# Two self-attentions: in PE's turn the score matmuls come ahead of the reciprocals' product and the transposition of the normalised tile

## The reference

```python
def _layernorm(x, axis=-1, eps=1e-05):
    m = jnp.mean(x, axis=axis, keepdims=True)
    v = jnp.var(x, axis=axis, keepdims=True)
    return (x - m) / jnp.sqrt(v + eps)
...
        q = _apply_rope(q, cos, sin)
        k = _apply_rope(k, cos, sin)
...
        scores = jnp.einsum('bhqd,bhkd->bhqk', q, k) / jnp.sqrt(jnp.float32(HEAD_DIM))
        causal = jnp.where(jnp.tril(jnp.ones((S, S), jnp.float32)) == 0, -1000000000.0, 0.0)
        scores = scores + causal
        attn = jax.nn.softmax(scores, axis=-1)
        out = jnp.einsum('bhqk,bhkd->bhqd', attn, v)
...
    x = x + _L0_attn_ref(_layernorm(x, axis=-1), L0_attn_wq, L0_attn_bq, L0_attn_wk, L0_attn_bk, L0_attn_wv, L0_attn_bv, L0_attn_wo, L0_attn_bo)
    x = x + _L0_xattn_ref(_layernorm(x, axis=-1), ctx_1024, ctx_1024, L0_xattn_igate_kernel, L0_xattn_igate_bias, L0_xattn_fgate_kernel, L0_xattn_fgate_bias, L0_xattn_outnorm_scale)
    x = x + _L0_ffn_ref(_layernorm(x, axis=-1), L0_ffn_sW1, L0_ffn_sb1, L0_ffn_sW2, L0_ffn_sb2, L0_ffn_rW1, L0_ffn_rb1, L0_ffn_rW2, L0_ffn_rb2, L0_ffn_gW, L0_ffn_gb)
    x = x + _L1_attn_ref(_layernorm(x, axis=-1), L1_attn_Wq, L1_attn_Wk, L1_attn_Wv, L1_attn_Wo)
    x = x + _L1_xattn_ref(ctx_1024, _layernorm(x, axis=-1), L1_xattn_gamma_x, L1_xattn_beta_x, L1_xattn_gamma_l, L1_xattn_beta_l, L1_xattn_Wq, L1_xattn_Wkv, L1_xattn_Wo)
    x = x + _L1_ffn_ref(_layernorm(x, axis=-1), L1_ffn_phi, L1_ffn_W, L1_ffn_b)
```

## Time and profile before

| | |
|---|---|
| median of 3 runs | 2063.2 us (2062.44 to 2063.45) |
| the profiled execution | 2060.2 us, span of its instructions 2058.1 us |
| self-attention of layer 0 | about 57 to 256 us; PE busy 176.09, DVE 170.35, ACT 156.30, POOL 130.45 of 199 us |
| self-attention of layer 1 | about 824 to 1031 us; PE busy 179.08, DVE 148.60, ACT 161.14, POOL 98.68 of 207 us |
| busy over the whole span | PE 1863.2, DVE 1458.5, ACT 1446.9, POOL 1123.8 us |

### The profile page before, as it was taken

How to read it: one execution, slowest core, us unless ns; L and a number is a source line. 1 busy time by engine, 2 the same in 40 slices (tenths; PEclk the granted TensorE clock), 3 DMA queues, 4 the chain that set the end, 5 groups by cost and what they waited for, 6 DMA issues and landing times. The chain is left out here.

```text
span 2058.1 us, 62588 instructions
## 1 busy us (share of the span) xinstructions
PE 1863.2 (91%) x23443; PEld 1475.0 (72%) x23505; DVE 1458.5 (71%) x3895; ACT 1446.9 (70%) x4203; POOL 1123.8 (55%) x1453
## 2 busy tenths in 40 slices
PE   5899798699999998889879999767999999999998
PEld 3566565577777776566568888656888888888787
DVE  7799768666566665677756666578777777777567
ACT  5688767688888887688768888566666666666532
POOL 5677447688888888545333333147444544445520
PEclk9999999899999999899999999899999999999999
DMA  3011010322222222000011111100000000000101
GB/s 98 28 48 41 13 33 3 83 73 73 74 72 77 73 73 62 23 2 2 2 34 32 33 33 33 58 26 4 5 15 18 5 16 5 16 15 3 56 8 39
DMA packets 60619, 72.47 MB, mean 35 GB/s; under 512 B 10264, under 2 KB 38696, under 8 KB 60064
## 3 DMA queue, kind: packets, MB, share of 16 engines
q1 hardware_dynamic: 51104, 64.29, 10.5%
q10 hardware_dynamic: 9216, 4.20, 0.7%
HBM read 51.43 MB, written 4.44 MB: 27 GB/s over the span
## 5 line engine op out<-in xcount | busy, mean ns | idle before, releaser
L1094 POOL TENSOR_TENSOR ff_hl<-ff_hid,ff_hh 128x512 fp32r<-128x512 f32 x272 | 350.2, 1302 | 69.1 <-ACT ff_hh L1335 61.9
L1954 POOL TENSOR_TENSOR sm_zsum<-sm_zsum,sm_logits 128x512 f32<-128x512 f32 x120 | 154.6, 1289 | 271.2 <-ACT sm_logits L1980 269.5
L1257 DVE TENSOR_TENSOR ff_hid<-ff_p_b,ff_gates 128x512 f32<-128x512 f32 x240 | 164.4, 686 | 148.6 <-ACT ff_p_b L1324 146.4
L1997 ACT ACTIVATE sm_sT<-sm_p_s 128x512 f32<-128x512 f32 x128 | 69.5, 595 | 217.3 <-PE sm_p_s L1790 217.3
L613 ACT ACTIVATE at_pr<-at_p_s,at_small 128x64 f32<-128x64 f32 x512 | 154.9, 329 | 61.1 <-DVE at_small L499 61.1
L1335 ACT ACTIVATE ff_hh<-ff_hid 128x512 fp32r<-128x512 f32 x272 | 169.9, 625 | 39.1 <-DVE ff_hid L1257 38.9
L1324 ACT ACTIVATE ff_p_b<-ff_p_h,early_b 128x512 f32<-128x512 f32 x240 | 156.9, 654 | 19.3 <-PE ff_p_h L1151 18.0
L1966 POOL TENSOR_TENSOR sm_logits<-sm_logits,sm_peak 128x512 f32<-128x512 f32 x128 | 163.1, 1296 | 12.5 <-ACT sm_comb L2015 11.9
L1804 PE MATMUL sm_p_l<-g_phi,g_xnT 128*128 128x256 f32 x512 | 142.3, 404 | 26.5 <-ACT sm_logits L2025 25.3
L582 POOL TENSOR_TENSOR at_kblk<-at_kT,early_heads 128x512 f32<-128x512 f32 x128 | 131.7, 1049 | 28.9 <-PE at_p_s L479 26.7
L1838 PE MATMUL sm_p_y<-sm_w,sm_sT 128*32 128x128 f32 x4096 | 125.4, 274 | 9.1 <-ACT sm_combT L1987 8.4
(11 more groups left out here) (305 smaller groups left out, 5610.1 us busy)
## 6 DMA issues: line engine op xcount, KB each, us to landing
ff_gates<-kept_gates SPq DMA_DIRECT2D x120, 256.0 KB, 3.1
xa_kturn<-xa_ksin SPq DMA_DIRECT2D x128, 64.0 KB, 2.0
at_turned<-at_terms SPq DMA_DIRECT2D x64, 64.0 KB, 1.9
sm_w<-in_w_soft SPq DMA_DIRECT2D x8, 512.0 KB, 3.5
early_whole<-in_L_ffn_rW SPq DMA_DIRECT2D x30, 128.0 KB, 2.6
early_xs<-in_x ACTq DMA_DIRECT2D x32, 64.0 KB, 1.9
ld_ctx<-in_ctx ACTq DMA_DIRECT2D x32, 64.0 KB, 2.1
x_kept<-early_xs SPq DMA_DIRECT2D x1, 2048.0 KB, 7.4
```

Source lines behind the costliest of these rows:

```text
L1094: eng.tensor_tensor(hl[:, q, :], hid[:, q, :], hh[:, q, :].bitcast(F32), ALU.subtract).then_inc(h_split, 1)
L1257: dve.tensor_tensor(h, p_b[c % 2][:, :], gates[:, n % GR, :], ALU.mult).then_inc(scaled, 1)
L1954: pool.tensor_tensor(z, z, logits[:, j % RING_L, :, :], ALU.add).then_inc(summed, 1)
```

## The change

In PE's turn the block of the scores moves in front of the block of L460 and that of L300. No instruction, wait or buffer is added or removed; every wait stays with its block. It is in the code of both layers.

```diff
                     mm.then_inc(v_done, 1)
-                k, v = t, u
-                if has(k):
-
-
-                    pe.wait_ge(inverted, k + 1)
-                    if has(k - 1):
-                        pe.wait_ge(oT_made, k)
-                    pe.matmul(p_o[:, P:2 * P], inv[:, v % 2, :, :].rearrange("p h d -> p (h d)"), g["ident"][:, :],
-                              start=True, stop=True).then_inc(inv_turned, 1)
-                k, v = t - 3, (u - 1) % 2
-                if has(k):
-                    if has(t - 2):
-                        pe.wait_ge(x_made, t - 1)
-                    norm.pe_transpose(pe, k, v, p_y[:, P:2 * P])
                 k, v = t + 2, (u + 2) % R
                 if has(k):
...
                     mm.then_inc(s_done, 1)
+                k, v = t, u
+                if has(k):
+
+
+                    pe.wait_ge(inverted, k + 1)
+                    if has(k - 1):
+                        pe.wait_ge(oT_made, k)
+                    pe.matmul(p_o[:, P:2 * P], inv[:, v % 2, :, :].rearrange("p h d -> p (h d)"), g["ident"][:, :],
+                              start=True, stop=True).then_inc(inv_turned, 1)
+                k, v = t - 3, (u - 1) % 2
+                if has(k):
+                    if has(t - 2):
+                        pe.wait_ge(x_made, t - 1)
+                    norm.pe_transpose(pe, k, v, p_y[:, P:2 * P])
```

## The result

The changed kernel takes 2079.46 us (median of five runs, 2074.03 to 2082.24), the kernel before, run beside it, 2063.45: ratio 1.0066, 95% interval 1.0045 to 1.0087. The profiled execution took 2077.89 us with a span of 2075.8.

A forecast was written before the change was run, and what follows sets the result against it. A loop of DVE and POOL, not PE, was taken to set the steady turns. Terms 14.7 + 1.4 - 2.4 = +13.7 us, on the 2063.2 us median, gave 2077 us, range 2067 to 2080.

The forecast's parts named there:

- The mechanism and its price: Layer 1: earlier scores let L582 start before L290 and hold it; +0.64 us in each of 23 turns, +14.7 us.
- the length of the score block: PE, start of L475 to end of L479: taken as 1.39 us, so scores end 4.90 us behind L499.
- in hand: Layer 1: L582 could start at 5.08 us behind L499 but POOL frees at 5.47, a margin of 0.39 us.
- rival A: L290 still comes first or is not held; only the first turns' gain remains, 2060.8 us, no change; chance 0.11.
- The two early norm turns: Layer 1, two turns with a norm ahead of the steady ones: L290 held, 0.7 us each, +1.4, bounds 0 and +1.4.
- The first turns: Both layers, before the norm begins: DVE waits for scores, so earlier scores gain; together -2.4 us, bounds -1.3 and -3.0.
- Rival B: PE is the pace, and its wait for L523 leaves every turn: 16.3 us faster, 2047 us; chance 0.04.
- Rivals C and D: L290 held in only 10 to 20 turns, 2067 to 2075, chance 0.07; or by both L582 halves, 2100, chance 0.03.

The follow-up runs named there:

- three buffers: Kernel before, PE's old order, with three kblk buffers instead of two in layer 1, so L582 is free earlier: 2072.96 us, ratio 1.0055.
- late L290: Changed kernel with layer 1's L290 moved behind L499 and L500 of the next turn; with L582 waiting for L290: 2050.91 us.
- layer 0's wait: Changed kernel with L572 in layer 0 and L582 in layer 1 both made to wait for L290: 2056.14 us.

## Why the prediction was right

**The mechanism and its price.** L582 loses its wait, starts 0.13 ahead of L290 (measured 0.14), L290 takes 0.98 (0.984), the turn is 6.50 (6.51). Each came as worked out, and the runs show it from both sides. 2077 was forecast, 2079.46 measured: inside the stated 2067 to 2080, and 0.5 above the 2074 to 2079 of the mechanism alone.

**A term that was mis-sized: the length of the score block.** I took 1.39 us from the start of L475 to the end of L479, and had the scores end 4.90 us behind L499. They end 943.20-938.09=5.11 behind it. The row of L475 in the earlier trace rows is the second of two matmuls, the record of the first is missing; it stands as x2 in the earlier trace rows, where L479 is this row of before's timeline, with the L499 behind it:

```profile
67.47 1.09 PE L479 MATMUL at_p_s<-at_kblk,at_qT 64*64 64x512 f32 x8
...
68.63 0.69 DVE L499 TENSOR_REDUCE at_small<-at_p_s 128x8 f32<-128x512 f32 x1 [1.98 <-PE at_p_s L479]
```

The block is 67.47+1.09-66.95=1.61 us. The weight loads had it. The kernel before, timeline of PE's weight loads in the turn of the earlier trace rows, and the same of after, where two loads stand beside one matmul:

```profile
936.38 0.21 PEld L475 LDWEIGHTS at_p_s<-early_bias,early_pick 128*128 128x128 bf16 x2
937.01 0.21 PEld L479 LDWEIGHTS at_p_s<-at_kblk,at_qT 64*64 64x64 f32 x8 [0.42 <-issue]
```

```profile
967.58 0.13 PEld L461 LDWEIGHTS at_p_s<-early_bias,early_pick 128*128 128x128 bf16 x2 [1.07 <-issue]
...
967.83 0.38 PE L461 MATMUL at_p_s<-early_bias,early_pick 128*128 128x512 bf16 x1 [1.18 <-DVE at_oT L523]
```

So L582 had 5.47-5.11-0.18=0.18 us in hand, not 0.39. It was enough, but rival A was nearer than the 0.39 us made it look.

**The two early norm turns.** One was held (L290 1.06, turn 6.35 against 5.65), the other was not: its scores ended only 5.31 behind L499, and L582 came second. +0.7 instead of +1.4, inside the bounds.

**The first turns.** The two turns bound by the scores are 5.03 and 5.20 us, not "5.0 or a little less"; the longer block is a part of that. And the first of them had been 74.16-68.63=5.53 before, not the 5.66 of the earlier trace rows. Over five turns layer 0 gained about 1.2 us, and it gave that back in the turn ahead of them. The windows of after, from the first L499 on, show it (PEclk is the third number from the end):

```profile
63.20:66.60 3.40, 1.20 (x16) 0.84 (x12) 3.01 (x7) 2.42 (x17) 3.04 (x5) 1.00 0.00 0
66.60:70.00 3.40, 3.20 (x12) 0.79 (x13) 0.21 (x1) 0.98 (x4) 0.34 (x2) 0.50 0.14 40
```

PE was busy 1.20 us of the first window, and in the second the granted clock was 0.50, which is 1.2 GHz. The turn took 6.34 us; in the trace of before the same turn was at full clock and took 5.03. Over the other traces it lies between 5.27 and 6.35 us where layer 0 has the old order (6.33 with three buffers), and between 5.03 and 6.35 with the new one. So this belongs to the execution, not to the change.

**Layer 1 as a whole.** Forecast 14.7+1.4-0.9=+15.2 us, measured +14.9. The steady turns gave 14.7, as forecast; the early norm turns gave 0.7 instead of 1.4 and the first turns -0.5 instead of -0.9. That two misses almost cancel is luck. Rival B is out: earlier scores did not shorten a steady turn in any run in which POOL's loop stood. Rivals C and D did not come.

**The whole sum.** The span of the profiled execution grew from 2058.1 to 2075.8, by 17.7 us: 14.9 in layer 1, nothing in layer 0 (forecast -1.5), 4.8 in the stage right behind layer 0, and -2.1 in the stage right behind layer 1 (295.7 us, before 297.8). The forecast of this execution was +13.7. So the price of layer 1 is borne out, and the median's closeness to 2077 is in part chance: the parts that were not forecast, 4.8 and -2.1 us in that execution, are about as large as the 2.5 us that the median is off by.

**What the trace doesn't tie to the change.** The stage right behind layer 0 (its tiles begin with ml), which no edit touches, took 4.8 us longer in the profiled execution: from the start of its first instruction to that of its last 253.6 to 376.6 us, before 253.6 to 371.7. Windows over it, before and then after:

```profile
260.00:375.00 115.00, 90.55 (x1517) 66.97 (x1510) 82.55 (x467) 74.45 (x294) 70.57 (x160) 0.94 0.06 16
```

```profile
260.00:380.00 120.00, 96.24 (x1522) 70.16 (x1514) 82.65 (x467) 74.91 (x294) 70.79 (x160) 0.88 0.06 15
```

The same matmuls take 5.7 us more of PE at a mean granted clock of 0.88 instead of 0.94. Two experiments had the longer stage too (late L290 in layer 1, with and without the wait), the others not. Why the clock falls at another place in one execution than in another stays open, and so does how much of the scatter of the runs, several us for each kernel, comes from it. A median here can carry some us that have nothing to do with the edit, as the 2056.14 of layer 0's wait shows; for differences of that size the turns of the traces decide.

## What to carry to other kernels

When a wait is made to end earlier, look at every engine that waits for it, and at what its next instruction will lie over: here the instruction that came free went in front of a DVE instruction on the path and cost 16 us. What helped in this kernel was to start the long GpSimd instruction behind the short DVE one that the loop needs, by a wait on it (the whole 0.64 us of a turn came back), or to cut it in pieces (0.43 came back). Then look at what it lies over next: with the late L290 it was the copy L520. And before moving PE's work, ask what sets the turn: the same reordering was worth nothing, -16 or +21 us, by what else was on the path.

## What was not expected

- Of two bias matmuls one had no record in most turns, while both weight loads did. The start of a PE block is safer read from the weight loads: 0.22 us in a turn of 5.86.
- Hold and duration match to 0.01 us over leads of 0.07 to 0.49 us, and L290 gets between two GpSimd instructions that follow each other without a gap. In the one turn where it started 0.08 us ahead of the second it was held by that one too.
- DVE's subtraction and reduction of 128x512 kept their 0.68 us beside the same GpSimd instruction that stretched a 128x128 copy from 0.23 to 0.78.
